# A two-sided graph convolution over 16 batches: every adjacency chunk split in two parts, with the shift made a batch earlier

## The reference, cut to what matters

```python
h = jnp.maximum(_layernorm(x, axis=-1), 0.0)
A_list = [adj, adj, shifted, adj^T, adj^T, shifted^T, eye]            # 7 relations
HW  = einsum('bnf,rfo->rbno', h, W[:, :F]) + einsum('rd,rdo->ro', W_edges, W[:, F:])
AHW = einsum('rbnm,rbmo->rbno', A, HW)
out = x + max over r of AHW + b
```

## Time and profile before

| | before |
|---|---|
| median of 3 runs | 214.75 us (213.66 to 214.75) |
| profiled execution | 213.96 us, span 212.1 us |
| mean granted TensorE clock | 0.999 of full speed |
| PE, DVE, ACT, POOL busy | 204.4, 175.5, 160.7, 89.4 us |
| moved by DMA | 51.06 MB, mean 241 GB/s |

### The profile page before, as it was taken

How to read it: one execution, slowest core, us unless ns; L and a number is a source line. 1 busy time by engine, 2 the same in 40 slices (tenths; PEclk the granted TensorE clock), 3 DMA queues, 4 the chain that set the end, 5 groups by cost and what they waited for, 6 DMA issues and landing times.

```text
span 212.1 us, 3382 instructions
## 1 busy us (share of the span) xinstructions
PE 204.4 (96%) x894; PEld 147.0 (69%) x894; DVE 175.5 (83%) x411; ACT 160.7 (76%) x432; POOL 89.4 (42%) x138
## 2 busy tenths in 40 slices
PE   7998989999999999999999999999999999999992
PEld 7556457766777677777777777777767777776771
DVE  3487849999799897979889797988989799997755
ACT  4887889696969869696987969697696968785230
POOL 3041232955256615437261633624473272726200
PEclk9999999999999999999999999999999999999999
DMA  5999999897988959497894959689794959833101
GB/s 161 336 364 371 348 343 281 214 311 205 338 223 306 293 132 400 107 378 196 262 331 141 391 104 385 172 266 292 200 388 88 384 122 299 245 99 53 49 2 49
DMA packets 33746, 51.06 MB, mean 241 GB/s; under 512 B 1872, under 2 KB 11328, under 8 KB 33728
## 3 DMA queue, kind: packets, MB, share of 16 engines
q1 hardware_dynamic: 31152, 46.53, 64.1%
q0 software_dynamic: 2304, 4.20, 12.5%
q10 hardware_dynamic: 272, 0.13, 0.2%
HBM read 46.65 MB, written 4.19 MB: 240 GB/s over the span
## 4 chain that ended last, share of the span: by engine, by line
PE 82%; DVE 6%; DMA 6%; issue 2%; SPq 1%; ACT 1%; POOL 0%; DVEq 0%; ACTq 0%; POOLq 0%
PE bank_p L848 11%; PE bank_p L850 9%; PE bank_p L849 9%; DMA x_sb<-in_x_dram 6%; PE bank_g L808 5%; PE bank_gT L787 5%; PE bank_gT L799 4%; PE bank_g L819 4%; PE bank_g L813 4%; PE bank_gT L793 4%; PE bank_g L812 4%; PE bank_gT L792 4%; PE bank_p L729 3%; PE bank_p L838 3%; PE bank_p L737 2%; DVE best L629 2%
## 5 line engine op out<-in xcount | busy, mean ns | idle before, releaser
L324 POOL TENSOR_TENSOR a_lo<-adj_sb,a_hi 128x512 fp32r<-128x512 f32 x14 | 18.2, 1298 | 52.7 <-DVE h_lo L598 50.6
L629 DVE TENSOR_TENSOR best<-bank_p,best 128x512 f32<-128x512 f32 x48 | 33.2, 691 | 7.5 <-PE bank_p L850 6.3
L626 DVE SCALAR_TENSOR_TENSOR best<-bank_p,c_col,best 128x512 f32<-128x512 f32 x32 | 24.0, 750 | 9.3 <-ACT best L473 8.4
L454 ACT ACTIVATE gT_hi<-bank_gT 128x512 fp32r<-128x512 f32 x16 | 9.6, 597 | 29.1 <-PE bank_gT L799 28.2
L310 POOL DMA_DIRECT2D x_bias<-in_xT_dram x16 | 14.0, 876 | 34.5 <-DMA x_bias<-in_biasT_dram 34.5
L436 ACT ACTIVATE h<-x_sb,shift,rstd 128x128 f32<-128x128 f32 x60 | 24.7, 487 | 2.2 <-DVE shift L578 2.2
L407 ACT ACTIVATE a_hi<-adj_sb 128x512 fp32r<-128x512 f32 x42 | 25.9, 622 | 0.2 <-DMA adj_sb<-in_adj_dram 0.2
L420 ACT ACTIVATE aT_hi<-adjT_sb 128x512 fp32r<-128x512 f32 x42 | 25.9, 624 | 0.0
L592 DVE TENSOR_TENSOR aT_lo<-adjT_sb,aT_hi 128x512 fp32r<-128x512 f32 x28 | 23.9, 891 | 0.0
L330 POOL TENSOR_TENSOR aT_lo<-adjT_sb,aT_hi 128x512 fp32r<-128x512 f32 x14 | 22.0, 1569 | 1.2 <-ACT aT_hi L420 1.2
L318 POOL TENSOR_TENSOR o_sb<-best,x_bias 128x512 f32<-128x512 f32 x15 | 20.0, 1332 | 5.9 <-DMA x_bias<-in_xT_dram 3.0
(11 more groups left out here) (126 smaller groups left out, 517.4 us busy)
## 6 DMA issues: line engine op xcount, KB each, us to landing
adj_sb<-in_adj_dram SPq DMA_DIRECT2D x15, 1024.0 KB, 5.7
adjT_sb<-in_adjT_dram SPq DMA_DIRECT2D x15, 1024.0 KB, 7.7
x_bias<-in_biasT_dram SPq DMA_DIRECT2D x16, 256.0 KB, 5.9
x_bias<-in_xT_dram POOLq DMA_DIRECT2D x16, 256.0 KB, 4.7
x_sb<-in_x_dram SPq DMA_DIRECT2D x15, 256.0 KB, 8.0
out_dram<-o_sb SPq DMA_DIRECT2D x15, 256.0 KB, 5.8
adj_sb<-in_adj_dram SPq DMA_DIRECT2D x4, 256.0 KB, 5.3
adjT_sb<-in_adjT_dram SPq DMA_DIRECT2D x4, 256.0 KB, 5.2
```

The source lines that it names most:

```text
L629: op = nc.vector.tensor_tensor(best[q][:, :], product, best[q][:, :], ALU.max)
```

## The change

- From batch 2 on all four chunks are split. There is no plain matmul left there; each direction has four hi·hi, then four lo·hi, then four hi·lo matmuls. `h_hi` and `h_lo` grow from 128x384 to 128x512. The copies to `summed` become copies to `a_hi` / `aT_hi`.
- VectorE keeps two subtractions per direction (chunks 0 and 1), GpSimd has two (chunks 2 and 3).
- `std`, `rstd` and `shift` get two buffers. `std_of(b+2)` and `scale_and_shift(b+2)` are done in batch `b`: on ScalarE before `split_gT(b)` instead of after `split_adjT(b+1)`, on VectorE behind `split_hT_lo(b)`; before, `scale_and_shift(b+1)` stood ahead of `split_gT_lo(b)`.
- First batches: `load_x(3)` goes ahead of `load_adj(2)`, `variance(3)` behind `split_g_lo(1)`, `product(0, 2)` behind the first product of `g`.

```diff
-WHOLE = (0,)
-SPLIT = (1, 2, 3)
-NS = len(SPLIT)
-ND = NS - 1
+ND = 2
+NG = 2
+NS = ND + NG
...
+            load_x(3)
             load_adj(2)
             load_adjT(2)
             load_bias(1)
-            load_x(3)
...
             def split_adj_last(b):
-                pool.wait_ge(ahi_ready, (b - FIRST + 1) * NS)
-                nc.gpsimd.tensor_tensor(a_lo[q][:, ND, :], adj_sb[q][:, C - 1, :], a_hi[q][:, ND, :].bitcast(F32),
+                for c in range(ND, NS):
+                    pool.wait_ge(ahi_ready, (b - FIRST) * NS + c + 1)
+                    nc.gpsimd.tensor_tensor(a_lo[q][:, c, :], adj_sb[q][:, c, :], a_hi[q][:, c, :].bitcast(F32),
...
+                if 2 <= b < B - 2:
+                    std_of(b + 2)
                 split_gT(b)
...
-                if b + 2 < B:
-                    std_of(b + 2)
...
                 split_adjT_lo(b)
-                if b + 1 < B:
-                    scale_and_shift(b + 1)
                 split_gT_lo(b)
                 split_hT_lo(b)
+                if b + 2 < B:
+                    scale_and_shift(b + 2)
...
             def aggregate_T(b):
-                for c in WHOLE:
-                    nc.tensor.matmul(bank_gT[:, 0:N], h[q][:, c, :], adj_sb[q][:, c, :],
-                                     start=(c == WHOLE[0]), stop=False)
+                for c in range(C):
+                    pe.wait_ge(ahi_ready, (b - FIRST) * NS + c + 1)
+                    nc.tensor.matmul(bank_gT[:, 0:N], h_hi[q][:, c, :], a_hi[q][:, c, :], start=(c == 0), stop=False)
                 pe.wait_ge(hlo_ready, b - FIRST + 1)
...
-                product(0, 2)
                 pe.wait_ge(crow_ready, 1)
                 pe.wait_ge(wlo_ready, 3)
                 pe.wait_ge(glo_ready, 1)
                 passes(5, bank_of[5][:, 0:N], start=True)
+                product(0, 2)
```

More of the change, by code:

```diff
@@ L418, in split_adjT @@
                     act.wait_ge(g_psum, b - 1)
[L419 to L420 removed]
+                for c in range(C):
+                    nc.scalar.activation(aT_hi[q][:, c, :], adjT_sb[q][:, c, :], ACT.Copy,
                                          accum_out=sums[q][:, 1, c:c + 1]).then_inc(aThi_ready, 1)
[L422 to L425 removed]
             def make_h(b):
@@ L492, in _ @@
             for c in range(HALF, C - 1):
-                last = nc.scalar.activation(h[0][:, c, :], x_sb[0][:, c, :], ACT.Relu, bias=shift[:, c:c + 1],
-                                            scale=rstd[:, c:c + 1])
+                last = nc.scalar.activation(h[0][:, c, :], x_sb[0][:, c, :], ACT.Relu, bias=shift[0][:, c:c + 1],
+                                            scale=rstd[0][:, c:c + 1])
             last.then_inc(h_ready, 1)
@@ L782, in aggregate_T @@
                 q = b % 2
[L783 to L784 removed]
+                pe.wait_ge(hhi_ready, b - FIRST + 1)
                 pe.wait_ge(gTlo_ready, b)
[L786 to L788 removed]
+                for c in range(C):
+                    pe.wait_ge(ahi_ready, (b - FIRST) * NS + c + 1)
+                    nc.tensor.matmul(bank_gT[:, 0:N], h_hi[q][:, c, :], a_hi[q][:, c, :], start=(c == 0), stop=False)
                 pe.wait_ge(hlo_ready, b - FIRST + 1)
[L790 to L800 removed]
+                for c in range(C):
+                    nc.tensor.matmul(bank_gT[:, 0:N], h_lo[q][:, c, :], a_hi[q][:, c, :], start=False, stop=False)
+                for c in range(C):
+                    if c < ND:
+                        pe.wait_ge(alo_ready, (b - FIRST) * ND + c + 1)
+                    else:
+                        pe.wait_ge(alo_last_ready, (b - FIRST) * NG + c - ND + 1)
+                    last = nc.tensor.matmul(bank_gT[:, 0:N], h_hi[q][:, c, :], a_lo[q][:, c, :],
+                                            start=False, stop=(c == C - 1))
                 last.then_inc(gT_psum, 1)
@@ L804, in aggregate @@
                 q = b % 2
-                pe.wait_ge(adjT_in[q], times(b))
                 pe.wait_ge(best_done, b * NBEST)
-                for c in WHOLE:
-                    nc.tensor.matmul(bank_g[:, 0:N], h[q][:, c, :], adjT_sb[q][:, c, :],
-                                     start=(c == WHOLE[0]), stop=False)
-                for i in range(NS):
-                    pe.wait_ge(aThi_ready, (b - FIRST) * NS + i + 1)
-                    nc.tensor.matmul(bank_g[:, 0:N], h_hi[q][:, i, :], aT_hi[q][:, i, :], start=False, stop=False)
-                    nc.tensor.matmul(bank_g[:, 0:N], h_lo[q][:, i, :], aT_hi[q][:, i, :], start=False, stop=False)
-                for i in range(NS):
-                    if i < ND:
-                        pe.wait_ge(aTlo_ready, (b - FIRST) * ND + i + 1)
-                    else:
-                        pe.wait_ge(aTlo_last_ready, b - FIRST + 1)
-                    last = nc.tensor.matmul(bank_g[:, 0:N], h_hi[q][:, i, :], aT_lo[q][:, i, :],
-                                            start=False, stop=(i == NS - 1))
+                for c in range(C):
+                    pe.wait_ge(aThi_ready, (b - FIRST) * NS + c + 1)
+                    nc.tensor.matmul(bank_g[:, 0:N], h_hi[q][:, c, :], aT_hi[q][:, c, :], start=(c == 0), stop=False)
+                for c in range(C):
+                    nc.tensor.matmul(bank_g[:, 0:N], h_lo[q][:, c, :], aT_hi[q][:, c, :], start=False, stop=False)
+                for c in range(C):
+                    if c < ND:
+                        pe.wait_ge(aTlo_ready, (b - FIRST) * ND + c + 1)
+                    else:
+                        pe.wait_ge(aTlo_last_ready, (b - FIRST) * NG + c - ND + 1)
+                    last = nc.tensor.matmul(bank_g[:, 0:N], h_hi[q][:, c, :], aT_lo[q][:, c, :],
+                                            start=False, stop=(c == C - 1))
                 last.then_inc(g_psum, 1)
```

114 lines of the change are left out of this document (51 added, 63 removed).

## The result

Six runs of each kernel on one chip: the changed kernel takes 208.55 us in the median, the kernel before 214.54 us. The ratio is 0.9726, 95% interval 0.9697 to 0.9755: 2.7% faster. Four of the six lie at 208.36 to 208.62 us, two at 211.5 and 211.8; the ratios here and in experiments 6, 8 and 11 leave such long executions out (the medians do not), and experiment 8 looks into one. The forecast was 211.5 us, range 207.5 to 215.3. The profiled execution takes 208.36 us (span 206.6), against 213.96 (212.1) of the one before.

A forecast was written before the change was run, and what follows sets the result against it. TensorE was taken to bound the kernel from batch 3 on. Terms of −4.4, +0.7 and +0.9 sum to −2.8 us, 213.96 to 211.2 us on the profiled execution; forecast 211.5 us, range 207.5 to 215.3.

The forecast's parts named there:

- −4.4 for TensorE: Batches 3 to 15: split matmuls replace one plain chunk per direction, 0.34 us less per batch, 13 batches, −4.4 us.
- +0.7 for late biases: Steady part: late bias delays two GpSimd `aT_lo`, blocking VectorE's `aT_lo` and `shift`; two such batches at 0.4, +0.7 us.
- +0.9 at the start: First batches: 1.6 us gained before batch 2 is lost to stalls in it; batch 3 starts at 48.9, not 47.99.
- the forecast's own 210 to 213: Whole kernel: the range of the main forecast without its rivals, 210 to 213 us, chance 0.45.
- rival 1: First batches: the start's gain is kept as stalls in batch 2 shrink; −6.1 us, 207.9 us; chance 0.22.
- the lock: VectorE and GpSimd subtractions hold each other up; steady part: GpSimd held, VectorE by 0 to 0.3 us, inside 0.8 slack.
- the regrouping costs nothing: TensorE, steady part: ordering matmuls as hi·hi, lo·hi, hi·lo costs nothing, as every matmul had its own weights before.
- rival 2: Steady part: `finish` slips between VectorE's two `aT_lo`; `g_lo` misses its slack by about 0.4 us each batch; 215.7 us; chance 0.18.
- My reason against the rival: Steady part: the L302 before `finish` were themselves held behind VectorE, so `finish` can't slip in.
- The two added subtractions a batch: GpSimd, steady part: second `a_lo` is free, second `aT_lo` makes part sums 1.23 us later, which TensorE doesn't see.
- rival 3: Steady part: the loop through GpSimd and the bias load becomes the bound, 12.9 us a batch, 222.7 us; chance 0.08.
- Rival 4: TensorE: splitting isn't cheaper or the plain matmul was hidden; only the start counts, 213.5 to 215 us; chance 0.07.

The follow-up runs named there:

- experiment 6: The changed kernel with the start's order alone put back to that of the kernel before: 209.03 us, ratio 0.9739 to the kernel before.
- experiment 8: The changed kernel run again with no edit; its profiled execution was a long one of 211.53 us: median 208.94 us, ratio 0.9729 to the kernel before.
- experiment 11: The changed kernel with one unused tile of 32 bytes a partition declared ahead of `eps`: 211.2 us, ratio 0.9770 to the kernel before.
- experiment 4: The kernel before with the new start order, new places of deviation and shift, two buffers for each, nothing more split: 211.95 us, ratio 0.9900.
- experiment 5: The kernel before with unused second buffers for `std`, `rstd` and `shift`, moving later tiles by 96 bytes: 213.14 us, ratio 0.9943.
- experiment 10: The changed kernel with GpSimd waiting at batch 1, `finish` behind its `a_lo`, bias DMA behind part sums, `adjT` load ahead of store: 206.17 us, ratio 0.9623.
- experiment 3: The changed kernel with the start's order, standard deviation and shift put back, leaving splitting alone: 215.0 us, ratio 1.0050 to the kernel before.
- experiment 7: The changed kernel with GpSimd's bias DMA issued behind `aT_lo` and the part sums: 216.61 us, ratio 1.0109 to the kernel before.
- experiment 2: The changed kernel, no edit, on another chip: 211.3 us median, ratio 0.9861 to the kernel before.
- experiment 1: The kernel before, no edit, on another chip: 215.71 us in its one profiled run.

## Why the prediction was right, and where its sizes were off

**The sum.** Forecast: −4.4 for TensorE, +0.7 for late biases, +0.9 at the start, −2.8 us in all, 211.5 us. Measured between the two profiled executions: −5.4 from batch 3 on and −0.1 before it. The 208.55 us lie inside the stated range, but outside the forecast's own 210 to 213, and next to the 207.9 of rival 1, for which the lower end had been set and whose mechanism didn't come. So the direction and the bound (TensorE's own work in the steady part) were foreseen, but that the range held is in part luck. What used up the room left for rival 1 was 1.3 us (13 × 0.10) from where a tile lies, for which the prediction had no term, 0.8 (13 × 0.06) from the distance of the split matmuls and 1.0 at the start, against 0.3 more lost to the lock than allowed for.

**TensorE, steady: mechanism right, size 0.42 instead of 0.34 us a batch.** The runs take it apart. With the tiles where the changed kernel has them, splitting takes 12.185 (experiments 4, 5) down to 11.79 (experiment 10): 0.40 us. One direction takes 112.52 − 109.59 = 2.93 us before and 109.94 − 107.21 = 2.73 after. I had priced the three new matmuls at the old distance of 0.230 and they, and the nine old ones, come at 0.2275. What makes those 2.5 ns each is open: the tiles' sizes and the grouping changed together. It also means that "the regrouping costs nothing" was never tested by itself. Then 0.10 us come from where the weights lie, which no row of the profile before could show and the prediction didn't think of. And the two engines' holding each other (the lock) gives back 0.08 us on average, the pair of late batches included: 12.29 − 0.40 − 0.10 + 0.08 = 11.87.

**The lock in the steady part.** I said that GpSimd would be held and VectorE hardly, and gave the lock in every batch as rival 2. In the changed kernel it happens in about every other batch, 1.05 us on VectorE, of which 0.08 reach TensorE: a slack of nearly 1.0 us, where I had worked out 0.8. My reason against the rival, that `finish` can't slip in since the part sums are held, was half right: `finish` meets the pair whenever the part sums are over, or nearly, when the pair begins, in most batches of experiments 3 and 7. One thing that makes them late is the bias DMA ahead of GpSimd's `aT_lo`; experiment 7 took that away. The price of rival 2, 0.4 us a batch, fits neither case: the collision it describes costs 0.08 us in the changed kernel, and the longer one of experiment 7 (3.0 us, 1.7 more than alone) costs 0.7 (12.5 against 11.8).

**The shift a batch ahead.** The prediction saw that two PSUM reads now stand between `aT_lo` and the shift, but gave the new place no price. That is the step it valued too low, though it didn't move the sum: without it the splitting gives 1.005 instead of 0.974. It isn't an optimisation beside the splitting but what makes the splitting pay: where nothing more is split, the period is the same with it (experiment 4) and without it (experiment 5).

**The late bias, +0.7 us: right, with one such batch instead of two.** One pair of batches takes 24.2 instead of 23.7 us in the profiled execution, so +0.5; the long one of the two is 12.38 us (timeline).
```profile
166.31 0.87 POOL L315 DMA_DIRECT2D x_bias<-in_xT_dram  x1 [1.51 <-DMA x_bias<-in_biasT_dram]
...
166.92 2.82 POOL L337 TENSOR_TENSOR aT_lo<-adjT_sb,aT_hi 128x512 fp32r<-128x512 f32 x2
...
168.40 1.90 DVE L595 TENSOR_TENSOR aT_lo<-adjT_sb,aT_hi 128x512 fp32r<-128x512 f32 x1
...
175.31 0.50 PE L836 MATMUL bank_p<-sumsT,c_rows 32*128 32x512 f32 x3 [0.51 <-DVE g_lo L616]
```
GpSimd waits 1.51 us for the bias; in the other steady batches of this execution it waits at most 0.32. Its two `aT_lo` then meet VectorE's, the first of which takes 1.90 us, and TensorE waits 0.51 us for `g_lo`. Experiment 2 shows the same once: a wait of 2.49 us for the bias (DMA instruction at 120.71), VectorE's first `aT_lo` 2.04 us, a period of 12.51. In experiment 10, where `aT_lo` and the part sums stand ahead of the DMA instruction, its waits of up to 2.0 us lengthen no period. This is the course that the prediction gave. The `shift` behind it is held too, 0.54 us. Why the bias is late in that batch is open.

**The start, +0.9 us; −0.1 measured (on one pair of executions, and 0.0 on that of experiments 1 and 2).** The course was as foretold: both engines at `a_lo(2)` from 31.3, VectorE's pair 3.5 us, TensorE waiting for the bests, then 0.4 us for ScalarE's `sumsT` where I expected `g_lo`. Two terms were late by too much: batch 2 starts at 33.1 and not 33.7, and the bias lands by 35.6 and not 36.9. So rival 1's time nearly came out (207.9), but not by its mechanism: the start was not kept. The prediction also missed that an earlier bias is dangerous: in experiment 8 it lets GpSimd in front of the shift, and that execution is 3.2 us longer. By the Trainium skill ("SBUF — State Buffer", Who interferes with whom) two such instructions exclude each other for the whole instruction, whoever issued first. The trace agrees, and goes beyond it: the shift of 0.16 us took 2.71, as long as GpSimd's whole pair (2.79) and not one instruction of it.

**GpSimd.** The two added subtractions a batch are hidden, as forecast; rival 3 (12.9 us) is refuted by 11.87. Rival 4 is refuted by the 2.73 us.
